# A recommender's attention kernel: low one-hots on ScalarE, low rows by half tile, high one-hots for two steps at once

## The reference

```python
item_emb = concatenate([table_i1[item[:, 0]], table_i2[item[:, 1]], table_i3[item[:, 2]]], axis=1)
ub = concatenate([table_i1[rec_his[:, :, 0]], table_i2[...1], table_i3[...2]], axis=2)   # [B, L, 96]
mask = rec_his[:, :, 0] == 0
q = broadcast_to(item_emb[:, None, :], ub.shape)
att_in = concatenate([q, ub, q - ub, q * ub], axis=-1)
h = att_in @ w_att1.T + b_att1
score = (h @ w_att2.T + b_att2)[..., 0]                    # no non-linearity: one vector per user
score = where(mask, 0.0, score)
browse = einsum('bl,ble->be', score, ub)
feat = concatenate([item_emb, browse, user_emb], axis=-1)
x = dice(feat @ w1.T + b1); x = dice(x @ w2.T + b2)        # dice uses mean and variance over the batch
out = sigmoid(x @ w3.T + b3)
```

## Time and profile before

| | us |
|---|---|
| runs of the kernel before | 1501.13, 1508.28, 1511.05; median 1508.28 |
| the profiled execution: its span, first to last instruction | 1506.3 |

### The profile page before, as it was taken

The page is one execution under the profiler, slowest core; times in us unless marked ns, Lnnn a source line. Parts: engine busy times, 40 slices in busy tenths (PEclk is TensorE's granted clock), DMA queues, the critical chain, the costliest instruction groups (busy, mean ns, idle before and its releaser), DMA issues.

```text
span 1506.3 us, 66273 instructions
## 1 busy us (share of the span) xinstructions
PE 1299.2 (86%) x27007; PEld 1186.0 (79%) x27007; DVE 1405.9 (93%) x1397; ACT 758.1 (50%) x1729; POOL 1188.4 (79%) x1671
## 2 busy tenths in 40 slices
PE   5688989889898988889898998989899898988864
PEld 4577878888887988788788888878888887888761
DVE  6699999999999999899999999999999999999945
ACT  5554455555445555454555554454555545452217
POOL 3588788888888888788888888888888888888830
PEclk8899999999999999999999999999999999999966
DMA  3566676666667666666766666666676666565820
GB/s 51 111 137 127 127 143 133 141 144 141 124 137 143 130 146 140 127 133 133 143 131 142 146 141 134 130 137 132 143 143 140 141 132 138 131 149 133 153 54 1
DMA packets 517508, 194.38 MB, mean 129 GB/s; under 512 B 485445, under 2 KB 493237, under 8 KB 517245
## 3 DMA queue, kind: packets, MB, share of 16 engines
q1 hardware_dynamic: 499654, 162.61, 53.5%
q10 hardware_dynamic: 15448, 26.51, 6.7%
q0 software_dynamic: 2144, 1.36, 0.8%
HBM read 8.45 MB, written 1.44 MB: 7 GB/s over the span
## 4 chain that ended last, share of the span: by engine, by line
POOL 72%; issue 15%; PE 3%; DVE 3%; POOLq 3%; ACT 2%; DMA 1%; ACTq 1%; SPq 0%; DVEq 0%
POOL score L439 24%; POOL score_r L448 14%; POOL score L444 11%; POOL parts L449 9%; POOL parts L452 6%; POOL item_rows L417 4%; POOL parts L445 3%; POOL user_rows L425 2%; DVE score_j L1026 1%; DVE onehot_lo L1012 1%; ACT scores_b L775 1%; PE sel L727 1%; DMA hiT<-onehot_hi 1%; POOLq L437 1%; POOLq L443 1%
## 5 line engine op out<-in xcount | busy, mean ns | idle before, releaser
L560 PE MATMUL wsum_ps<-scaled_lo,onehot_hi 100*128 100x75 bf16 x12288 | 535.0, 201 | 81.5 <-DVE scaled_lo L1038 80.2
L543 PEld LDWEIGHTS sel<-scoretab,hiT 128*128 128x128 bf16 x12288 | 495.8, 99 | 121.6 <-DMA hiT<-onehot_hi 59.2
L543 PE MATMUL sel<-scoretab,hiT 128*128 128x75 bf16 x12288 | 534.5, 201 | 63.1 <-DMA hiT<-onehot_hi 43.9
L1038 DVE TENSOR_TENSOR scaled_lo<-onehot_lo,parts 100x3744 bf16<-100x3744 bf16 x256 | 539.0, 2105 | 34.4 <-POOL parts L452 26.4
L560 PEld LDWEIGHTS wsum_ps<-scaled_lo,onehot_hi 100*128 100x128 bf16 x12288 | 486.1, 99 | 106.3 <-DVE scaled_lo L1038 101.7
L439 POOL TENSOR_TENSOR score<-score_j 100x16 f32<-100x16 f32 x256 | 386.6, 1510 | 156.6 <-DVE score_j L1026 155.7
L768 ACT ACTIVATE wsum_ring<-wsum_ps 128x300 f32<-128x300 f32 x512 | 215.5, 421 | 525.7 <-PE wsum_ps L560 497.2
L1026 DVE TENSOR_REDUCE score_j<-sel 100x24 f32<-100x600 f32 x512 | 395.5, 772 | 21.0 <-PE sel L543 21.0
L994 DVE TENSOR_TENSOR onehot_hi<-digits,iota_hi 100x1920 bf16<-100x1920 bf16 x256 | 296.1, 1157 | 3.4 <-PE wsum_ps L560 3.3
L775 ACT ACTIVATE scores_b<-acc 128x512 bf16<-128x512 f32 (+1 forms) x318 | 255.4, 803 | 50.0 <-issue 22.7
L448 POOL TENSOR_TENSOR score_r<-score,parts 100x16 f32<-100x16 f32 x256 | 207.3, 810 | 20.0
(11 more groups left out here) (168 smaller groups left out, 724.0 us busy)
## 6 DMA issues: line engine op xcount, KB each, us to landing
scoretab<-scores_b SPq DMA_DIRECT2D x384, 93.8 KB
weightsum<-wsum_ring ACTq DMA_DIRECT2D x128, 125.0 KB
weightsum<-wsum_ring ACTq DMA_DIRECT2D x64, 150.0 KB
raw<-in_r_rec_his_dram SPq DMA_DIRECT2D x32, 150.0 KB
hiT<-onehot_hi SPq DMA_TRANSPOSE x256, 3.8
x_rows<-x_tile SPq DMA_DIRECT2D x14, 100.0 KB
scores_b<-x_rows SPq DMA_DIRECT2D x1, 1400.0 KB
item_rows<-in_L_rec_table_i_dram,ids_now POOLq DMA_INDIRECT x51
```

The costliest lines, as they stand in the source:

```text
L543: mm = pe.matmul(sel[:, 2 * (s % 2) + q, (c % 4) * W:(c % 4 + 1) * W] .rearrange("p (j v) -> p j v", j=NF), hiT[0:HJ, s // 2 % 4, g * POSP ...
L560: mm = pe.matmul(wsum_ps[:, s % 2, b * W:(b + 1) * W].rearrange("p (j v) -> p j v", j=NF), hi_columns(ring_slot(n), g), scaled_lo[:, n % 2 ...
L1038: ins = dve.tensor_tensor(scaled_lo[:, n % 2, :, :, :].rearrange("p q i (u d) -> p (q i) u d", d=2), onehot_lo[:, n % 2, :, :, :].rearrang ...
```

## The change

- `onehot_low` moves from VectorE to ScalarE. It was a compare of low digits with 0..25 for a whole step (100 x 1248). It becomes Relu(sel * 2/FAR + 1) for each slot, straight from the 600 numbers in `sel` that `pick` reads: 1 at the right low value and 0 elsewhere. It waits for the pick of the same slot; TensorE's `read_scores` now waits for it too before it writes the `sel` banks anew. It stands first in ScalarE's slot.
- The one-hot loses the spare column of each id; a single spare column is left at the end (U = 76 in place of 78), so `scale` writes 100 x 3648 elements where it wrote 100 x 3744.
- `lo_rows`: the low digit and its square are computed once for half a tile, when the digits arrive (`low_rows`, two instructions), and each step copies its part with one instruction (100 x 96) where it had two of 100 x 48.
- `onehot_high` makes two steps in one instruction (100 x 3840), in even steps, and the ring has eight buffers. `hi_ready` counts pairs.
- Two small memsets are added in the prologue.

```diff
-    HJ, U, W = HB + NF * HI, NF * LP, NF * LO
+    HJ, W = HB + NF * HI, NF * LO
+    U = W + 1
-    RING = 6
+    RING = 8
...
-        def ring_slot(n):
-            return n % 5 if n < STEPS - 1 else RING - 1
-        def sums_before(k, n):
-            return 2 * k - (8 if 5 <= n < STEPS - 1 else 10 if n < 5 else 2 * STEPS - 2)
+        def ring_slot(n):
+            return n % RING
+        def ring_used(k):
+            return not isinstance(k, int) or k >= RING
...
@@ SyncE, turn_hi
-                await_ge(hi_ready, k + 1)
+                await_ge(hi_ready, t * (STEPS // 2) + n // 2 + 1)
@@ TensorE, read_scores
                     pe.wait_ge(score_ready, k - 1)
+                    pe.wait_ge(lo_ready, k - 1)
@@ TensorE, add_scores
-                                       scaled_lo[:, n % 2, g, i % 3, :].rearrange("p (j v) -> p j v", j=NF)[:, :, 0:LO],
+                                       scaled_lo[:, n % 2, g, i % 3, 0:W].rearrange("p (j v) -> p j v", j=NF),
@@ ScalarE, task "digit"
-                            act.wait_ge(lo_ready, (t - 1) * STEPS + 8 * hb + 8)
+                            act.wait_ge(lo_rows_ready, (t - 1) * STEPS + 8 * hb + 8)
...
+                        rows = low_rows[:, hb, :, :, :].rearrange("p g j i -> p j g i")
+                        act.activation(rows[:, :, :, 0], src, ACT.Identity, bias=centre[:, :])
+                        ins = act.activation(rows[:, :, :, 1], src, ACT.Square, bias=centre[:, :])
@@ ScalarE
+            def onehot_low(t, s):
+                k = t * SLOTS + s
+                n, g0 = s // 2, (s % 2) * 8
+                act.wait_ge(score_ready, k + 1)
+                if s % 2 == 0 and not (isinstance(k, int) and k < 4):
+                    act.wait_ge(scaled_ready, t * STEPS + n - 1)
+                act.activation(onehot_lo[:, n % 2, g0:g0 + 8, 0:W].rearrange("p (q c) u -> p q c u", q=2),
+                               sel[0:POS, 2 * (s % 2):2 * (s % 2) + 2, 0:4 * W].rearrange("p q (c u) -> p q c u", u=W),
+                               ACT.Relu, bias=one[:, :], scale=2.0 / FAR).then_inc(lo_ready, 1)
@@ ScalarE, lo_rows
-                if ring_used(k, n):
-                    act.wait_ge(wsum_full, sums_before(k, n))
-                act.activation(rows[:, :, :, 0], low, ACT.Identity, bias=centre[:, :])
-                act.activation(rows[:, :, :, 1], low, ACT.Square, bias=centre[:, :]).then_inc(lo_rows_ready, 1)
+                if ring_used(k):
+                    act.wait_ge(wsum_full, 2 * (k - RING) + 2)
+                act.activation(onehot_hi[0:POS, ring_slot(n), :, 1:1 + 2 * NF],
+                               low_rows[:, hb, g0:g0 + PER, :, :].rearrange("p g j i -> p g (j i)"), ACT.Copy
+                               ).then_inc(lo_rows_ready, 1)
@@ ScalarE, slot
             def slot(t, s, odd, last=False):
                 here = tasks_of(t)
+                onehot_low(t, s)
@@ VectorE, onehot_high
+                if ring_used(k):
+                    dve.wait_ge(wsum_full, 2 * (k + 1 - RING) + 2)
+                dve.tensor_tensor(onehot_hi[0:POS, ring_slot(n):ring_slot(n) + 2, :, HB:]
+                                  .rearrange("p s g (j v d) -> p (s g) j v d", j=NF, d=2),
+                                  digits[:, hb, g0:g0 + 2 * PER, :, :].unsqueeze(3)
+                                  .to_broadcast([POS, 2 * PER, NF, HI // 2, 2]),
...
@@ VectorE, scale
-                dve.wait_ge(lo_ready, k + 1)
+                dve.wait_ge(lo_ready, 2 * k + 2)
@@ VectorE, step
-                if n + AHEAD < STEPS:
+                if n % 2 == 0 and n + AHEAD < STEPS:
                     onehot_high(t, n + AHEAD)
-                elif not last:
+                elif n % 2 == 0 and not last:
                     onehot_high(t + 1, n + AHEAD - STEPS)
-                onehot_low(t, n)
```

More of the change, by code:

```diff
@@ L69, in build @@
         onehot_hi = sb("onehot_hi", [POSP, RING, PER, HJ], BF16)
-        onehot_lo = sb("onehot_lo", [POS, 2, PER, NF, LP], BF16)
+        onehot_lo = sb("onehot_lo", [POS, 2, PER, U], BF16)
+        one = sb("one", [POS, 1])
         scaled_lo = sb("scaled_lo", [POS, 2, PER, 3, U], BF16)
@@ L77, in build @@
         parts = sb("parts", [POS, 2, PER, 3, 2], BF16)
-        digits = sb("digits", [POS, 2, 2, 2 * HALF, NF, 2], BF16)
+        digits = sb("digits", [POS, 2, 2 * HALF, NF, 2], BF16)
+        low_rows = sb("low_rows", [POS, 2, 2 * HALF, NF, 2], BF16)
         far_rows = sb("far_rows", [1, 3, LO], BF16)
@@ L801, in task @@
                         if kind == 1:
-                            act.wait_ge(hi_ready, (t - 1) * STEPS + 8 * hb + 8)
+                            act.wait_ge(hi_ready, (t - 1) * (STEPS // 2) + 4 * hb + 4)
                         else:
-                            act.wait_ge(lo_ready, (t - 1) * STEPS + 8 * hb + 8)
-                    src = (misc_b if kind == 1 else misc)[0:POS, 0:2 * NF * HALF]
-                    ins = act.activation(digits[:, hb, kind, :, :, :].rearrange("p g j d -> p j g d"),
-                                         src.rearrange("p (j g) -> p j g", j=NF).unsqueeze(3)
-                                         .to_broadcast([POS, NF, 2 * HALF, 2]), ACT.Copy)
+                            act.wait_ge(lo_rows_ready, (t - 1) * STEPS + 8 * hb + 8)
+                    src = ((misc_b if kind == 1 else misc)[0:POS, 0:2 * NF * HALF]
+                           .rearrange("p (j g) -> p j g", j=NF))
+                    if kind == 1:
+                        ins = act.activation(digits[:, hb, :, :, :].rearrange("p g j d -> p j g d"),
+                                             src.unsqueeze(3).to_broadcast([POS, NF, 2 * HALF, 2]), ACT.Copy)
+                    else:
+                        rows = low_rows[:, hb, :, :, :].rearrange("p g j i -> p j g i")
+                        act.activation(rows[:, :, :, 0], src, ACT.Identity, bias=centre[:, :])
+                        ins = act.activation(rows[:, :, :, 1], src, ACT.Square, bias=centre[:, :])
                 elif name == "item":
@@ L877, in lo_rows @@
                         act.wait_ge(task_copied, task_before(t, 3) + 1)
-                if ring_used(k, n):
-                    act.wait_ge(wsum_full, sums_before(k, n))
-                low = digits[:, hb, 0, g0:g0 + PER, :, 0]
-                rows = onehot_hi[0:POS, ring_slot(n), :, 1:1 + 2 * NF].rearrange("p g (j i) -> p g j i", i=2)
-                act.activation(rows[:, :, :, 0], low, ACT.Identity, bias=centre[:, :])
-                act.activation(rows[:, :, :, 1], low, ACT.Square, bias=centre[:, :]).then_inc(lo_rows_ready, 1)
+                if ring_used(k):
[3 more added lines that the diff above has]
+                               ).then_inc(lo_rows_ready, 1)
             def slot(t, s, odd, last=False):
                 here = tasks_of(t)
+                onehot_low(t, s)
                 if s in here:
@@ L1076, in _ @@
             dve.memset(offset[:, :], -float(MID) / LO).then_inc(bias_ready, 1)
+            dve.memset(one[:, :], 1.0).then_inc(bias_ready, 1)
             dve.memset(w2col[:, :], 0.0).then_inc(dve_tail_pre, 1)
@@ L1114, in _ @@
             dve.wait_ge(const_ready, 5)
-            for n in range(AHEAD):
-                onehot_high(0, n)
+            onehot_high(0, 0)
             mask_digits(1, DIGITS0 - 1)
```

30 lines of the change are left out of this document (5 added, 25 removed).

## The result

The changed kernel takes 1565.5 us (median of 4, 1562.5 to 1571.2) where the kernel before takes 1506.8 (median of 4, 1501.1 to 1511.1): a ratio of 1.040, interval 1.036 to 1.043. It is slower by 59 us where some 95 us of gain were forecast.

What follows compares the result with a forecast made beforehand. VectorE bounds the kernel now, TensorE after the change: 77.1 us a tile plus 2.5, 1.5 and 1.3 gives 82.4 against 87.65. With the end tiles, 97.5 us less: span 1408.8, median 1411, range 1375 to 1450 (chance 0.52).

Steps and rivals of the forecast that it cites:

- VectorE's share: VectorE: onehot_low goes, compares are joined, scale shortens; two steps cost 8.77 us instead of 10.42, 211 us over 128 pairs.
- The Relu's price: ScalarE: each of 512 new 600-element Relus from PSUM takes 0.77 us, 394 us of busy time.
- TensorE's work: TensorE becomes the bound: 74.5 us a tile, 77.1 with its uneven groups of four slots.
- the third coupling: TensorE's read waits for ScalarE's Relu behind earlier copies: 3.3 us against VectorE's 2.6; 1.3 us a tile with other items.
- the low digits: ScalarE: the low digits now need two instructions per half tile, some 10 us in all.
- The first coupling: GpSimd's adds against VectorE: odd steps late by 0.26 us; gathers in steps 1 to 3 cost 2.5 us a tile.
- the second coupling: Transposed one-hots have 6.0 us instead of 8.7 before their pick and need 5.1 to 8.0: 1.5 us a tile.
- costed at nothing: Items said to cost nothing: ring of eight, scale's and the Relu's buffer waits, low digits' wait, joined hi_ready, two prologue memsets.
- C: Rival, slower: a two-step loop over four engines closes through Relu, lo_rows and late transposes, deciding from 6.5 us landing; 1538; chance 0.08.
- B's form on GpSimd: Form of rival B (1450 to 1493, chance 0.20): joined compares and late odd steps cost 0.7 us a pair, giving 1444.
- D: Rival, no change: the couplings eat 5 us a tile more than forecast, 87.3 us a tile, giving 1493; chance 0.08.
- The three signs that were to show the forecast wrong: Relu over 0.95 us, joined compare at one element a cycle (4 us), or waits for transposed one-hots past 150 us.

Runs made afterwards that it cites:

- the kernel with all four mends: Changed kernel with Relu last in the slot, low rows contiguous, single compares and a lead of three steps: 1424.0 us, ratio 0.947 to the kernel before.
- a longer lead: Changed kernel with Relu last and contiguous low rows, plus low rows, high one-hots and transposes made three steps ahead, not two: 1437.3 us, ratio 0.954.
- the extra Relu: One more 150-element Relu ahead of each real one, into an unread tile, on the 1424.0 us kernel: 1450.9 us, ratio 0.964 to the kernel before.

## Why the prediction was wrong

**VectorE's share was right.** Joined compare 2.16 us busy (said 2.1), scale 2.05 (said 2.06), no onehot_low: 1405.9 - 1210.3 = 196 us, of 211 counted start to start. **The Relu's price was right:** 761 ns, said 770. The copy of low rows takes 291 ns, said 270 to 360. ScalarE's sum was 1040, said 1070.

**TensorE's work was counted about right, its waits were not.** Its weight loads take 1202.9 us where they took 1186.0, at a granted clock of 0.944 and 0.957. Within the loop they are busy 73.1 us a tile, and 70.4 in the kernel with all four mends, which goes with the 74.5 from start to start. But the loop runs from its first pick at 50.38 to the end of the last scale at 1515.70, 91.6 us a tile. The forecast was 82.4 for a middle tile and, with its two ends, (1402.4 - 97.5) / 16 = 81.6 on average: 10 us a tile were missing. In the kernel with all four mends the loop runs from 51.12 to 1361.13, 81.9 a tile. That this is so near 81.6 is in part luck: that kernel has another order, a longer lead and no join, and its VectorE (86%) is busier than its weight loads (82%), so that TensorE is not plainly its bound.

**The step that failed is the third coupling**, "a read waits for the Relu and not only for the pick". Its kind was right and its size was not. It followed the right chain, from a pick's end over Relu, copy of sums, split copy, split piece and read: 3.3 us where VectorE takes 2.6 between every second pair. By these figures alone that is 0.7 us in each of eight steps, 5.6 us a tile, if nothing hides it; the sum took 1.3 us for this and three other things, called it its least certain term, and gave no reason for so little. The runs show that the larger figure was the better one: moving the call to the slot's end is worth 85 us, 5.3 us a tile, and TensorE's waits for split copies rose by 118 us, 7.4 a tile. The chain also left out what the same slot holds besides: the low rows (0.17 us), a task's copy in some slots, and twice a tile the pair of low-row writes (2.46 us). The diff puts the call at the head of the slot, so all of these and the split copy stand behind an instruction that none of them needs. ScalarE's engine queue has no way around it: in the trace the copy of 711.34 starts only after the Relu of 710.21, which waited for a pick, though its own piece was done at 710.43. (The Trainium skill, PSUM — Partial Sum Buffer, Engine vs sequencer instructions, calls ScalarE's queue strictly first in, first out; the trace agrees: in these rows Relu, sums, low rows and split copy start in the program's order, at 710.21, 710.87, 711.17 and 711.34.) Before the change the same idling stood at the copy of sums, 497 us of it, and that copy was then as late as the sums were, not as the pick was. How the 85 us divide between the Relu's wait and its length is not parted by a run. With the Relu in the middle of the slot the wait is down to 64 us and some 44 us are still lost, so the Relu's length ahead of the split copy has about half of them, or a third if the fastest of that kernel's executions (1509.0) is taken.

**The second failed term is the low digits**, "some 10 us". They cost 101 us of ScalarE where one copy of the low digits of about 26 stood, and in stretches of 2.46 us from start to start, for which the sum had nothing. The nearest rows had 1.57 ns an element as the dearest; these writes take 4.1 to 4.4. Worth 43 us with the Relu first and 25 with it last.

**The first coupling was of the right kind and about the right size.** Said: an odd step late by 0.26 us. Found: 0.20 in the median and 0.38 on average with the low one-hots still on VectorE. The join's 21 us once TensorE's waits are smaller hold some of the second coupling too, since the waits for transposed one-hots fell with it. **The second was about right as well:** 1.5 us a tile, 24 us, for late transposed one-hots; the longer lead brings 18. In the changed kernel the join's cost is lost behind the greater wait; a longer lead was not tried there.

**Of what was costed at nothing,** scale's wait for the Relu is 1.1 us by its row in the groups. The ring costs up to 2 us by its own run, and not by its waits but ahead of the loop: VectorE's clearing of the larger ring takes 6.9 us where it took 5.2, and the first pick starts at 50.38 where it started at 48.80. That the one brings the other was not tried. The other items have no run.

**The rivals.** C gave 1538 and had the sign, and it had seen that low rows and transposes come to stand behind the Relu. SyncE's waits for the low rows do show it, in the changed kernel:

```profile
SPq L291 <- ACT onehot_hi L896: 145.4, 122, 4.2
SPq L289 <- ACT onehot_hi L896: 70.7, 27, 11.1
```

216 us in all, where the kernel before has 26. But it made the landing decide, and the landing's median is 4.0 us where 6.5 were asked for; TensorE's wait for these transfers grew by 5 us. The work that was late for TensorE was the split copy, which C put ahead of the Relu. B's form on GpSimd gave 0.7 us a pair; the join's whole cost was 0.16 to 0.17 (21 and 22 us over 128 pairs). D, three couplings eating all of the gain, was the closest in kind and stopped at no change. The three signs that were to show the forecast wrong (a Relu over 0.95 us, a compare of 4 us, 150 us of waits for transposes) all stayed away: they were the signs of wrong prices for single instructions. Two of the signs that were to show it right did not come: the weight loads stand at 77% of the span and not above 83%, and scale waits for GpSimd less than before, not more (11.5 us in all where it was 26.4). The one on picks waiting for TensorE, "some 80 us or more", was open at the top: 299.

**The account.** From 1565.5: Relu last -85.2, low rows in one piece -25.0, no join -20.9, a longer lead -10.4, to 1424.0. That is 141.5 of the 154 us between the result and 1411. Each figure depends on this order of the edits (low rows first would be 43 us), and the last three are no surer than the spreads given above. What makes up the last 13 is open. VectorE still waits 117 us for TensorE there, against 21 before, and the extra Relu shows that ScalarE's busy time goes on reaching the end at a fifth; how much of the 13 that is was not measured.

## What to carry to other kernels

When an instruction with a new wait is put on an engine's queue, cost it twice: what its own result makes late, and what stands behind it in the queue and needed neither its wait nor its length. Where the others wait for copies on the same engine, try it last in its slot, behind them; here one moved call was worth 85 us, nearly as much as the whole change was to bring. And when a chain comes out longer than the time it has, multiply the difference by how often it occurs before writing a small number for it. An edit that seems free or harmful is to be tried again after each mend: the join cost nothing in the changed kernel and 21 us once it was in order.

## What the hardware showed beyond the forecast

ScalarE's write into a bf16 tile, 384 elements each 12 bytes from the next, from PSUM with a bias by partition, took 1575 ns (Identity) and 1688 ns (Square), 1.17 and 1.29 us from start to start. Side by side the same 384 took 583 ns, 0.46 us from start to start. The copy of the high digits, 768 elements in pairs of 4 bytes, a pair each 12 bytes, took 827. So neither the distance alone nor the count makes the price; single 2-byte elements at that distance do (that copy has no bias, which was not tried apart; that it reads bf16 makes no difference, since the same copy from f32 took 856 in the kernel before). Which of the two (the half word or the distance) it needs was not tried apart.

The weight loads differ by 41 us between kernels with the same number of them: the mean granted clock was 0.944 in the changed kernel, 0.957 before, 0.967 in the best one, and 27007 weight loads took 1202.9, 1186.0 and 1162.2 us. Among these three the clock is highest where the weight loads fill most of the span (77%, 79%, 82%), but the kernel with the Relu in the middle of the slot breaks the row (79% at 0.941); whether the one brings the other was not tried. So up to 17 of the 59 us of loss may be the clock's share. Moving the one call brought the clock back to 0.956, so where it has a share, it came with the order.
